# Rolling half of each stage into an inner loop, and projecting the last image's values late, in a two-layer attention kernel

## The reference, cut to what matters

```python
def layer0(x, ...):                       # x: (4, 128, 4096)
    g, theta = einsum('ic,bcn->bni', g_w, x) + g_b, einsum('ic,bcn->bni', theta_w, x) + theta_b
    phi = einsum('ic,bcn->bin', phi_w, x) + phi_b[:, None]
    y = softmax(theta @ phi, axis=-1) @ g           # 4096 x 4096 scores, 64 channels inside
    return W_w @ y^T + W_b[:, None] + x
def layer1(x, ...):
    q, k, v = Wq x + bq, Wk x + bk, Wv x + bv        # 128 channels
    return x + (softmax(q^T k / sqrt(128), axis=-1) @ v)^T
return layer1(layer0(x))
```

## Time and profile before

| | |
|---|---|
| median of 3 runs | 3359.24 us (3358.44 to 3360.39) |
| the profiled execution | 3360.39 us, of which the span is 3358.6 us |
| granted TensorE clock, mean | 0.997 |
| busy share of TensorE (matmuls) | 98% |
| GpSimd | 89% |
| VectorE | 62% |
| ScalarE | 50% |

### The profile page before, as it was taken

How to read it: one execution, slowest core, us unless ns; L and a number is a source line. 1 busy time by engine, 2 the same in 40 slices (tenths; PEclk the granted TensorE clock), 3 DMA queues, 4 the chain that set the end, 5 groups by cost and what they waited for, 6 DMA issues and landing times.

```text
span 3358.6 us, 42499 instructions
## 1 busy us (share of the span) xinstructions
PE 3307.8 (98%) x13124; PEld 2104.5 (63%) x13124; DVE 2084.2 (62%) x3016; ACT 1672.2 (50%) x2249; POOL 2992.1 (89%) x1379
## 2 busy tenths in 40 slices
PE   8999999999999999999999999999999999999998
PEld 5555555556666665555666666555566767666675
DVE  5555555556767665555766766555576767767674
ACT  5455445554444445554444444455545454544444
POOL 6888899998889989998988989999898998999897
PEclk9999999999999999999999999999999999999999
DMA  1000000000000000000000000000000000000000
GB/s 53 23 20 26 23 26 26 26 26 13 23 16 20 20 13 26 26 26 27 13 23 16 20 20 20 20 26 26 26 20 20 13 26 13 16 13 16 13 13 10
DMA packets 36657, 70.40 MB, mean 21 GB/s; under 512 B 4048, under 2 KB 4048, under 8 KB 36432
## 3 DMA queue, kind: packets, MB, share of 16 engines
q1 hardware_dynamic: 36432, 67.62, 6.6%
HBM read 50.83 MB, written 16.78 MB: 20 GB/s over the span
## 4 chain that ended last, share of the span: by engine, by line
PE 84%; POOL 9%; issue 4%; DVE 2%; ACT 1%; DMA 0%; DVEq 0%; POOLq 0%; SPq 0%; ACTq 0%
PE acc_out L484 14%; PE rough L425 14%; PE acc_out L502 13%; PE scores L449 7%; PE scores L452 7%; POOL sums L299 7%; PE scores L454 5%; PE scores L458 5%; PE scores L455 5%; PE acc_out L472 2%; PE acc_out L470 2%; PE acc_out L471 2%; PE rough L408 2%; DVE piece_max L841 2%; PE acc_out L414 1%
## 5 line engine op out<-in xcount | busy, mean ns | idle before, releaser
L299 POOL TENSOR_TENSOR sums<-sums,probs 128x1024 f32<-128x1024 f32 x894 | 2133.6, 2387 | 157.9 <-ACT probs L758 107.2
L841 DVE TENSOR_REDUCE piece_max<-rough 128x1 f32<-128x512 f32 x2032 | 1316.0, 685 | 652.9 <-PE rough L425 648.7
L858 DVE TENSOR_TENSOR probs<-scores,shift_rows 128x1024 f32<-128x1024 f32 x512 | 626.8, 1224 | 563.0 <-PE scores L458 561.0
L758 ACT ACTIVATE probs<-scores 128x1024 f32<-128x1024 f32 x512 | 520.9, 1024 | 679.9 <-PE scores L452 674.4
L751 ACT ACTIVATE probs<-probs 128x1024 f32<-128x1024 f32 x512 | 539.5, 1054 | 481.3 <-DVE probs L858 481.0
L425 PE MATMUL rough<-keys_a,qry_a 128*128 128x512 f32 x2032 | 709.5, 417 | 29.9 <-DVE piece_max L841 24.1
L502 PE MATMUL acc_out<-probs,v_vals 128*128 128x512 f32 x1280 | 604.7, 595 | 0.0
L955 POOL TENSOR_TENSOR p_lo<-probs,p_hi 128x1024 fp32r<-128x1024 f32 x192 | 459.3, 2392 | 157.0 <-ACT probs L751 157.0
L425 PEld LDWEIGHTS rough<-keys_a,qry_a 128*128 128x128 f32 x2032 | 367.8, 188 | 361.9 <-DVE piece_max L841 241.3
L454 PE MATMUL scores<-qry_a,keys_a 128*128 128x512 f32 x1024 | 507.1, 495 | 1.3 <-issue 1.3
L449 PE MATMUL scores<-qry_a,keys_a 128*128 128x512 f32 x1024 | 434.1, 424 | 0.0
(11 more groups left out here) (89 smaller groups left out, 2598.1 us busy)
## 6 DMA issues: line engine op xcount, KB each, us to landing
x_q<-x SPq DMA_DIRECT2D x32, 256.0 KB, 2.7
x_res<-x SPq DMA_DIRECT2D x32, 256.0 KB, 3.0
mid<-mid_new SPq DMA_DIRECT2D x32, 256.0 KB, 2.3
x_kv<-mid SPq DMA_DIRECT2D x32, 256.0 KB, 2.7
x_q<-mid SPq DMA_DIRECT2D x32, 256.0 KB, 2.7
x_res<-mid SPq DMA_DIRECT2D x32, 256.0 KB, 3.1
out<-result SPq DMA_DIRECT2D x32, 256.0 KB, 2.1
x_kv<-x SPq DMA_DIRECT2D x24, 256.0 KB, 2.7
```

What stands on the lines that cost most here:

```text
L299: eng.tensor_tensor(sums[:, parity], sums[:, parity], probs[:, s % P_BUFS], ALU.add).then_inc(s_plus, 1)
L841: nc.vector.reduce_max(piece_max[:, t, c:c + 1], src, AX.X).then_inc(s_reduced, 1)
L858: nc.vector.tensor_tensor(probs[:, s % P_BUFS].rearrange("p (h c) -> p h c", c=QB), scores[:, s % 2].rearrange("p (h c) -> p h c", c=QB), ...
```

## The change

Three things are changed.

1. `run_stage` writes out blocks 0, 5, 6 and 7 of a stage, and puts blocks 1 to 4 into an inner loop of two trips with two blocks in its body. In stages 2 to 5 this loop is nested in the outer one. Block numbers of blocks 1 to 4 depend on the inner register.
2. `hold`, `hold_v` and `move_v` are gone. In stage 6 SyncE loads chunks 0 to 3 of image 3 once more, into `g_vals`, in block 54, and chunk 4 into `x_kv` in block 55. TensorE projects chunks 0 to 4 in groups 9 to 13 of block 55, and chunks 5 to 7, loaded into `g_vals` in block 56, in groups 9 to 11 of block 56. All go through the one free bank, so each projection waits until `take_v` has emptied it of the chunk before (`h_v`), and the first of each block waits for its load (`s_late`). `take_v` stands in ScalarE's program behind the group's exponentials.
3. The kernel is built with the default size of the scratch area for dynamic DMAs, in place of 2048.

```diff
+LATE_V_AT = 9
+LATE_V_FIRST = 5
...
-            for i in range(BLOCKS):
+            step(0, 0)
+            with eng.Fori(0, 2) as j:
+                step(2 * j + 1, 1)
+                step(2 * j + 2, 2)
+            for i in range(5, BLOCKS):
                 step(i, i)
...
+            def load_late(c, n):
+
+                settle(sp)
+                sp.dma_start(g_vals[:, 0:n * QB], mid[B - 1][:, c * QB:(c + n) * QB]).then_inc(s_late, 16)
...
+                if st.stage.prepares == "late" and st.i_known == BLOCKS - 2:
+                    load_late(0, LATE_V_FIRST - 1)
+                if st.stage.prepares == "late" and st.i_known == BLOCKS - 1:
+                    k_read(B * BLOCKS)
+                    load_kv(st, 1, LATE_V_FIRST - 1)
+                if st.stage.late_values and st.opens:
+                    sp.wait_ge(p_v, (B - 1) * BLOCKS + LATE_V_FIRST - 1)
+                    load_late(LATE_V_FIRST, BLOCKS - LATE_V_FIRST)
...
-                    if s == V_AT and stage.prepares in ("kv", "late"):
+                    if s == V_AT and stage.prepares == "kv":
...
+                    if stage.prepares == "late" and st.new_keys and LATE_V_AT <= s < LATE_V_AT + LATE_V_FIRST:
+                        c = s - LATE_V_AT
+                        if c == 0:
+                            pe.wait_ge(s_done, st.g + 2)
+                            pe.wait_ge(s_late, 16)
+                        else:
+                            pe.wait_ge(h_v, stage.made * BLOCKS + c)
+                        if c == LATE_V_FIRST - 1:
+                            pe.wait_ge(s_xkv, 16 * st.g + 32)
+                        src = cols(g_vals, c) if c < LATE_V_FIRST - 1 else x_kv[:]
+                        project_keys(free_bank, wt_v, src, p_v)
+                    if stage.late_values and st.opens and LATE_V_AT <= s < LATE_V_AT + BLOCKS - LATE_V_FIRST:
+                        c = s - LATE_V_AT
+                        if c == 0:
+                            pe.wait_ge(s_done, st.g + 2)
+                            pe.wait_ge(s_late, 32)
+                        else:
+                            pe.wait_ge(h_v, st.b * BLOCKS + LATE_V_FIRST + c)
+                        project_keys(free_bank, wt_v, cols(g_vals, c), p_v)
...
-            def hold_v(n, c, src):
-
-                act.wait_ge(p_v, n + 1)
-                copy(held(c), src).then_inc(h_hold, 1)
-
-            def move_v(g, c):
-
-                act.wait_ge(s_used, g * GROUPS + TPG * c + 2 + P_BUFS)
-                act.wait_ge(h_hold, c + 1)
-                copy(v_hi[:, c:c + 1], held(c)[:, TPG * KT:].unsqueeze(1))
-                copy(cols(v_vals, c), held(c)).then_inc(h_v, 1)
...
+                    if stage.prepares == "late" and st.new_keys and LATE_V_AT < s <= LATE_V_AT + LATE_V_FIRST:
+                        c = s - LATE_V_AT - 1
+                        take_v(stage.made * BLOCKS + c, c, free_bank)
+                    if stage.late_values and st.opens and LATE_V_AT < s <= LATE_V_AT + BLOCKS - LATE_V_FIRST:
+                        c = s - LATE_V_AT - 1 + LATE_V_FIRST
+                        take_v(st.b * BLOCKS + c, c, free_bank)
...
-    nc = bacc.Bacc("TRN2", target_bir_lowering=False, num_devices=1, dynamic_dma_scratch_size=2048)
+    nc = bacc.Bacc("TRN2", target_bir_lowering=False, num_devices=1)
```

More of the change, by code:

```diff
@@ L39 @@
 K_AT, V_AT = 11, 11
-MOVES_AT = ({6: 0, 8: 1, 10: 2, 12: 3, 14: 4}, {1: 5, 3: 6, 5: 7})
+LATE_V_AT = 9
+LATE_V_FIRST = 5
 NEXT_Q_AT = 14
@@ L132, in build @@
         g_first = v_vals[:, 0:N // 2]
-        hold = sb("hold", [P, N // 2])
         v_hi = sb("v_hi", [P, BLOCKS, TPG * KT], F32R)
@@ L182, in build @@
         s_xres = sem("s_xres")
-        h_hold = sem("h_hold")
+        s_late = sem("s_late")
         p_q, h_q, l_q = sem("p_q"), sem("h_q"), sem("l_q")
@@ L227, in settle @@
             eng.sem_inc(s_settled[eng], 1)
-        def held(c):
-            return cols((g_vals, hold)[c // 4], c % 4)
         def rd(ap):
@@ L358, in kv_read, with k_read @@
                 sp.wait_ge(p_v, chunks)
+            def k_read(chunks):
+                sp.wait_ge(h_k, chunks)
+            def load_late(c, n):
+                settle(sp)
+                sp.dma_start(g_vals[:, 0:n * QB], mid[B - 1][:, c * QB:(c + n) * QB]).then_inc(s_late, 16)
             def load_prep(st):
@@ L372, in load_prep @@
                     if not st.opens:
-                        (phi_read if kind == "phi" else kv_read)(made * BLOCKS + st.i)
+                        (phi_read if kind == "phi" else kv_read if kind == "kv" else k_read)(made * BLOCKS + st.i)
                     elif st.stage.prepared_before == "kv":
@@ L624, in block_program @@
                             pe.wait_ge(h_g, stage.made * BLOCKS + st.i + 1)
-                        if stage.prepares == "late":
-                            pe.wait_ge(h_hold, st.i + 1)
+                        if stage.prepares == "late" and st.new_keys:
+                            pe.wait_ge(h_v, stage.made * BLOCKS + LATE_V_FIRST)
+                        if stage.late_values and st.opens:
+                            pe.wait_ge(h_v, B * BLOCKS)
                         shift_row(st.g + 1, 1 - st.parity)
@@ L992, in block_program @@
                 for s in range(GROUPS):
-                    if stage.late_values and st.opens and s - 1 in MOVES_AT[1]:
-                        c = MOVES_AT[1][s - 1]
+                    if stage.late_values and st.opens and LATE_V_AT + 1 < s <= LATE_V_AT + 1 + BLOCKS - LATE_V_FIRST:
+                        c = s - LATE_V_AT - 2 + LATE_V_FIRST
                         split_v(st.b * BLOCKS + c, c)
@@ L1012, in block_program @@
                         split_v(stage.made * BLOCKS + st.i, st.i)
-                    if stage.prepares == "late" and st.new_keys and s - 1 in MOVES_AT[0]:
-                        c = MOVES_AT[0][s - 1]
+                    if stage.prepares == "late" and st.new_keys and LATE_V_AT + 1 <= s < LATE_V_AT + LATE_V_FIRST:
+                        c = s - LATE_V_AT - 1
                         split_v(stage.made * BLOCKS + c, c)
+                if stage.prepares == "late" and st.new_keys:
+                    split_v(stage.made * BLOCKS + LATE_V_FIRST - 1, LATE_V_FIRST - 1)
             run_all(pool, block_program)
```

## The result

The changed kernel takes 3389.09 us (median of 4 runs, 3387.98 to 3395.15); the kernel before took 3359.51 us beside it (3358.44 to 3360.39). The ratio is 1.0092, with a 95% interval of 1.0075 to 1.0109: slower, by 29.6 us. Its profiled execution took 3390.46 us with a span of 3388.7, which is 30.1 us more than the span before, 3358.6. The forecast was 3387.

What follows compares the result with a forecast made beforehand. TensorE, busy 98%, was taken to set the pace, each standstill adding to the end time. Terms 0.6 + 4.0 + 1.5 + 5.3 + 8.6 + 8.0 = 28.0 us gave a median of 3387 us, range 3371 to 3412.

Steps and rivals of the forecast that it cites:

- Register waits, 4.6 us: Blocks 1 to 4 of stages 0, 1, 6 and 7 swap constants for registers: 0.6 in layer 0, 4.0 in layer 1.
- The second register, 1.5 us: Blocks 1 to 4 of stages 2 to 5 depend on two registers: 0 to 4.6 us possible, 1.5 taken.
- The back edges, 5.3 us in layer 0 and none in layer 1: Inner loop's taken branches: 1.33 us lost at each of four layer 0 edges, layer 1 edges hidden.
- I take the measured 1.33 for each of the four layer 0 edges: TensorE's inner edges in layer 0 each cost what the outer loop's edge cost the array: 5.3 us.
- rival A: Inner body stays in TensorE's instruction store, four edges cost about 0.08 us: 23.0 us slower, 3382 us; chance 0.17.
- VectorE ... is hidden in either layer: VectorE's hold at a back edge costs 0, as its next shift is due only behind the next scores.
- The late projections, 16.6 us: TensorE stands still in blocks 55 and 56 for new waits: 8.6 us and 8.0 us.
- The hand-overs: Projections wait for ScalarE's `take_v` of the chunk before: 1.1, 3.9, 1.1, 2.5 us in block 55, 1.1, 2.5 in 56.
- The load: Block 56's 768 KB load, behind store and residual in SyncE's queue, lands at 2926.5 to 2927: TensorE waits 4.4 us.
- B: Two-register waits cost the full 4.6 us and layer 1 edges aren't covered: 3396 to 3413 us; chance 0.26.
- C: GpSimd sets layer 1's pace, so only layer 0 edges and 0.6 us remain: 3365 us, no change; chance 0.07.
- D: Faster: only TensorE's present idle time, 0.1 to 0.25 us in a layer 1 block, can be gained; chance 0.02.

Runs made afterwards that it cites:

- the seventh experiment: The changed kernel with the blocks of stages 6 and 7 written out, so that they have constants: 3384.42 us, ratio 1.0072 to the kernel before.
- the ninth experiment: The changed kernel with VectorE's inner loop bodies placed at the start of a fetch block: 3385.57 us, ratio 1.0080 to the kernel before.
- after: The changed kernel itself, with all three parts of the change: 3389.09 us, ratio 1.0092 to the kernel before.
- the third experiment: The changed kernel with the load of chunks 5 to 7 issued ahead of SyncE's wait for `s_done`, store and residual: 3382.10 us, ratio 1.0065 to the kernel before.
- fifth: The changed kernel with that load issued early and `take_v` put ahead of the exponentials and `make_k`: 3368.10 us, ratio 1.0026 to the kernel before.
- tenth: The changed kernel with the early load, the early `take_v` and VectorE's placed inner loops: 3362.63 us, ratio 1.0010 to the kernel before.
- the first experiment: The changed kernel with the inner loop taken out, all blocks of a stage written out, late projections kept: 3380.66 us, ratio 1.0063 to the kernel before.

## Why the prediction was right, and where it was not

The time was right by 2 us. Two of its terms, the register waits and the late projections, had the right mechanism. The two halves of the term for the back edges were wrong in opposite directions and nearly cancelled, and one effect, the lower clock, was not foreseen.

**Register waits, 4.6 us: right.** Blocks 1 to 4 of stages 6 and 7 last 58.15 to 58.19 us, the written-out ones 57.61 to 57.65: 8 x 0.54 = 4.3. In stage 1 the same four blocks gained 0.07 to 0.13, 0.5 in all. These two make 4.8, and the seventh experiment, which takes them out of stages 6 and 7, gave 4.7 back against the 4.0 to 4.3 of this term. The place was right too: the idle times ahead of the third pieces grew by 0.15 to 0.16 us each, in three places of a block.

**The second register, 1.5 us: somewhat too high.** In layer 1 it costs nothing that shows: with the edge mended (the ninth experiment) stage 2 lasts 479.2 us against 479.3. In layer 0 stages 3 and 5 gained 0.45 to 0.5 each in the profiled executions of after and of the third experiment, and 0 to 0.2 in those of the other kernels with the nested loops. Where they gained 0.45, the written-out blocks behind the loop, which have one register as before, are longer by as much as the looped ones (44.13 us, from 44.07), so the second register is not the cause of all of it, and the cause stays open. So 0 to 0.5 for the second register in place of 1.5, and 0.9 for what these stages gained; the low bound, that the sum of both is kept as one base, was near.

**The back edges, 5.3 us in layer 0 and none in layer 1: both halves wrong.** The step "I take the measured 1.33 for each of the four layer 0 edges" failed, and rival A was right about it: the inner body, up to 1,072 instructions of TensorE, was still there, and all eight edges held its sequencer for 0.22 to 0.24 us, the outer one, with some 5,800 instructions of code in its body, for 3.88. The step "VectorE ... is hidden in either layer" failed too. It was argued that the next shift is due only behind the next scores; but VectorE reaches its branch behind the shift of the last group, at 930.0, and its code is back at 933.5, when the work of the next block is due. Two misses cost 2.3 and 1.9 us, 4.2 together. In layer 0 the step held: three of the branches added in the ninth experiment went on only after 2.8 us there and cost nothing. In place of 5.3 + 0 the runs show 0 + 4.2. So the total was saved by luck: a sum with A's edges gives 3382, and a reader who had taken A and left VectorE hidden would have been 7 us low.

The section of the Trainium skill on this, Runtime: NRT & Kernel Launch, Instruction fetch mechanics, has two paragraphs. That on TensorE's instruction memory of 2048 instructions agrees with the trace (0.22 us with 1,072, 3.88 with 5,800); that on a window of two pages, which the prediction set beside its forecast, would have made all eight of TensorE's edges dear, and the trace contradicts it.

**The late projections, 16.6 us: right in kind, 3.6 too small.** The blocks grew by 14.43 and 13.16 over their neighbours; less eight projections of 0.92 that moved there from other blocks, that is 20.2. The early copy and the early load together take away 21.0, so both waits are the cause, shown and not argued.
- The hand-overs were priced at 8.6 and 3.6 us, 12.2 together. Idle time ahead of the six projections is 1.00 + 4.17 + 0.84 + 2.76 and 1.06 + 2.76, which is 12.6. The step by which they were found, the end of ScalarE's copy less the time at which TensorE would have been ready, held in each: forecast 1.1, 3.9, 1.1, 2.5, 1.1, 2.5.
- The load was priced at 4.4 and took 6.13. The step "it lands at 2926.5 to 2927", 3.9 to 4.4 us after its issue, was mis-sized: it landed after 5.58. The 1.2 us for the further 512 KB assumed the highest rate of the queues. Issued early, in the third, fifth and tenth experiments, the same load lands after 4.7 to 5.0 us; issued behind the store and the residual it takes 5.2 to 5.7, in six kernels. So even the early one takes 2.0 to 2.3 us more than a load of 256 KB, not 1.2, and the place behind the store and the residual adds to it.
- The lower clock was in no term. It is worth 1.5 of the 3.6 at least, the load 1.7, the hand-overs 0.4. Of 20.2 us, 18.7 are the waits above. That leaves 1.5 as the least that the two stretches of 6.83 us at 0.50 can have cost; since some 0.24 us of idle time ahead of each of the seven weight loads was there before, it is up to 3.2. The third experiment gives the load's own share: 7.26 us less in block 56 for a wait of 6.13. Nor is this part the same each time: in the first experiment, with four falls of the clock, blocks 55 and 56 held 2.7 us more than in the changed kernel for waits of the same length.

**The rivals.** B (loops dearer, 3396 to 3413) had the wrong reasons: neither the second register nor TensorE's edges in layer 1 cost more, and no edge cost 3.9. C (GpSimd sets the pace) is refuted: GpSimd's busy share fell to 88%, and the time that TensorE was idle in blocks 55 and 56 came back in full when the waits were taken away. D (faster) found nothing, and its bound was wrong: it took TensorE's time outside its busy time, 0.1 to 0.25 us in a layer 1 block, for all that could be gained, but writing out the outer loop gave 0.51 in each such block of stages 2 and 4, and 11.3 us in all. The busy time itself fell, from 59.65 to 59.29 us for the same matmuls, so it holds waits too.

The sum as measured in the profiled execution: registers 4.8, stages 3 and 5 0.9, VectorE's edges 4.2, late part 20.2, makes 30.1; the span grew by 30.1. (One sum of the prediction is off, and nothing rests on it: 28.0 - 5.0 - 1.5 - 6 is 15.5, which gives 3375 and not 3373 for the low end.)

## What to carry to other kernels

Where one engine is busy for 98%, price every new wait by what stands ahead of its releaser in the releaser's own order: both large losses here lay in the order of instructions on an engine that was half idle, and moving six lines of ScalarE's and three of SyncE's program gave back 21 of the 30 us. A loop costs in three coins, which have to be read one by one for each engine: register instructions at every wait (0.5 us in a block of 60), the edge itself (0.2 to 0.3 us, or 3 to 4, by how much code the body has and where it begins), and whether something behind the edge hides it, as in layer 0 and in stage 7, or not, as in stages 2 and 4. A wait of 6.13 us on TensorE cost 7.26, since its clock had fallen by the time the work came.

## What the runs showed of the hardware

- TensorE's granted clock fell to 0.50 (1.2 GHz) in, or just behind, idle times. With the wait of 5.8 to 6.2 us for the load it stayed there for 6.83 us in all six traces that have this wait; with that of 4.17 us for 6.83 us in one trace and for 3.41 in five; with 2.76 us for 3.41 us in five cases of twelve, and not at all in seven. One idle time of 2.06 us brought a fall, others of 2.09 to 2.17 brought none, so the length of the idle time alone doesn't decide. With all these waits gone (the fifth experiment) the clock stays at 1.00 in both blocks. The Trainium skill (Advanced Engine Details and Errata, Clock Domains) says that the clock of the array is gated to 1.2 GHz when idle; the trace agrees.
- One more stretch of 3.41 us at 1.2 GHz cost 1.5 to 1.7 us in a kernel's last block (70.9 to 71.1 us in six traces, 69.4 in six).
- VectorE's taken branch went on after 0.3 us or after 2.8 to 3.4 us with bodies of nearly one size (310 and 312 instructions). Where the body begins decided: with its place set, in the ninth and tenth experiments, all sixteen inner back edges went on within 0.3 to 0.4 us, while in each of the two kernels three of the eight added branches into the loops took 2.8 to 3.0.
- A hint for a back edge removed the stall there and was followed by one of 2.7 us in straight code behind the loop, at a higher price.
- A load of 768 KB landed after 4.7 to 5.0 us when it was issued early, behind one load of 256 KB, and after 5.2 to 5.7 right behind a store and a load of 256 KB each; one of 256 KB lands after 2.7.
